# Mamba-2 block and Hadamard feed-forward on one core: ACT's parts of two chunk steps one tile later, squares of a quad by halves, one Hadamard step a tile, dt later

## What is computed

```python
def mamba2(x):                                     # 1024 channels, 16 heads of 64, state of 128
    z, xBC, dt = split(x @ w_in)
    dt = softplus(dt + dt_bias)
    xBC = silu(conv4(xBC) + conv_b)                # causal, 4 taps
    y = ssd(xh * dt, dt * A, Bm, Cm) + xh * D      # Lmat = exp(segsum(dt * A))
    y = y * silu(z)
    y = y * rsqrt(mean(y * y) + 1e-5) * norm_w
    return y @ w_out

xn = layernorm(x)
hidden = fwht(silu(xn @ W1.T) * (xn @ W3.T))       # fwht over 2048, 1/sqrt(2048)
x = x + (xn + mamba2(xn)) + hidden @ W2.T
```

## Time and profile before

| | |
|---|---|
| median of 3 runs | 967.67 us (966.13 to 968.0) |
| profiled execution | 965.39 us, span 963.6 us |
| PE busy | 934.7 us, 97% |
| DVE busy | 555.8 us, 58% |
| ACT busy | 391.4 us, 41% |
| POOL busy | 276.1 us, 29% |

### The profile page before, as it was taken

One profiled execution on the slowest core, in us unless ns is written; L12 is line 12 of the kernel. 1 busy time (PEld: TensorE's weight loads), 2 busy tenths in 40 slices (PEclk: granted clock), 3 DMA queues, 4 the chain that ended last, 5 costly groups with the idle time before them and its releaser, 6 DMA issues.

```text
span 963.6 us, 13435 instructions
## 1 busy us (share of the span) xinstructions
PE 934.7 (97%) x5000; PEld 469.3 (49%) x5000; DVE 555.8 (58%) x955; ACT 391.4 (41%) x690; POOL 276.1 (29%) x354
## 2 busy tenths in 40 slices
PE   9899987989899999999999999999999999999998
PEld 4444443545344445555454445555445445555543
DVE  7876588875534756556532766566451666575421
ACT  6678874533323445233221434233222444343200
POOL 0000446352000116466110106565210104654410
PEclk9999999999999999999999999999999999999999
DMA  9798355434224335525223435436223435256123
GB/s 336 247 349 295 112 192 193 131 124 137 96 74 147 125 111 159 155 72 176 88 67 113 143 99 164 145 97 175 78 76 101 143 107 160 65 151 153 45 77 98
DMA packets 76208, 134.26 MB, mean 139 GB/s; under 512 B 7536, under 2 KB 20464, under 8 KB 74096
## 3 DMA queue, kind: packets, MB, share of 16 engines
q1 hardware_dynamic: 56640, 104.88, 34.1%
q10 hardware_dynamic: 19504, 28.53, 10.0%
HBM read 107.43 MB, written 25.95 MB: 138 GB/s over the span
## 4 chain that ended last, share of the span: by engine, by line
PE 67%; DVE 1%; DMA 1%; ACT 1%; issue 0%; DVEq 0%; ACTq 0%
PE ps L600 46%; PE ps L834 14%; PE ps L796 2%; PE ps L782 1%; PE ps L788 1%; PE ps L768 1%; DMA arena<-cs_rows 1%; PE ps L619 0%; PE ps L638 0%; PE ps L751 0%; PE ps L771 0%; DVE arena L1348 0%; DVE arena L1426 0%; ACT arena L1059 0%; DVE arena L1265 0%
## 5 line engine op out<-in xcount | busy, mean ns | idle before, releaser
L600 PE MATMUL ps<-xh,arena 128*128 128x512 f16 x1592 | 487.9, 379 | 3.4 <-DVE arena L1194 3.3
L600 PE MATMUL ps<-xl,arena 128*128 128x512 f16 x796 | 302.0, 379 | 0.0
L600 PEld LDWEIGHTS ps<-xh,arena 128*128 128x128 f16 x1592 | 158.3, 99 | 190.3 <-issue 5.9
L834 PE MATMUL ps<-arena 128*128 128x512 f16 x768 | 171.1, 379 | 0.0
L1443 POOL TENSOR_TENSOR arena<-arena 128x512 f16<-128x512 f32 x64 | 71.2, 1113 | 334.6 <-ACT arena L978 334.6
L1244 DVE SCALAR_TENSOR_TENSOR arena<-ps,cw,arena 128x511 f32<-128x511 f32 (+2 forms) x120 | 89.4, 747 | 66.9 <-ACT arena L968 65.0
L600 PEld LDWEIGHTS ps<-xl,arena 128*128 128x128 f16 x796 | 77.9, 98 | 88.7 <-issue 3.3
L834 PEld LDWEIGHTS ps<-arena 128*128 128x128 f16 x768 | 74.1, 98 | 91.2 <-issue 5.5
L978 ACT ACTIVATE arena<-arena 128x512 f16<-128x512 f32 x64 | 40.2, 629 | 141.3 <-DVE arena L1265 141.3
L1260 DVE SCALAR_TENSOR_TENSOR arena<-arena,ps 128x512 f32<-128x512 f32 x64 | 44.0, 687 | 77.3 <-ACT arena L973 77.0
L600 PE MATMUL ps<-wo_hi,arena 128*128 128x512 f16 x256 | 79.9, 384 | 3.6 <-DVE wo_lo L1333 3.4
(11 more groups left out here) (179 smaller groups left out, 1092.8 us busy)
## 6 DMA issues: line engine op xcount, KB each, us to landing
arena<-w_parts SPq DMA_DIRECT2D x198, 256.0 KB, 2.6
w_parts<-arena SPq DMA_DIRECT2D x66, 256.0 KB, 2.6
arena<-cs_rows ACTq DMA_DIRECT2D x16, 1024.0 KB, 5.7
arena<-w SPq DMA_DIRECT2D x24, 512.0 KB, 4.9
arena<-ecs_rows ACTq DMA_DIRECT2D x24, 256.0 KB, 6.9
arena<-x ACTq DMA_DIRECT2D x18, 256.0 KB, 3.4
w_mid<-arena SPq DMA_DIRECT2D x8, 512.0 KB, 3.5
arena<-w_mid SPq DMA_DIRECT2D x16, 256.0 KB, 2.6
```

The source lines that it names most:

```text
L600: ins = nc.tensor.matmul(out_ap, lhs(i, a), rhs(i, c), start=(i == 0 and s == 0), stop=(i == n - 1 and s == 2))
L834: ins = nc.tensor.matmul(bank(t), hw[a][:, i, t * P:(t + 1) * P], w2s[i % W2R][:, d, :], start=(i == 0 and s == 0), stop=(i == JF - 1 and ...
```

## The change

Six things, all in batch 0:

- `FIRST`: DT moves from behind Z0 to behind C2, DTL from behind C2 to behind Z1, SUM from behind C4 to behind Z2, ahead of C4.
- An SQ entry is now one half of a quad (two tiles), with its own place; halves of one quad stand one to three tiles apart.
- ACT's part of Y (the square of y) becomes a step of its own, YS, and ACT's part of N (y as fp16) becomes NS, each with its own places in batch 0: mostly one tile behind Y and N. In the other batches they stand at the places of Y and N.
- The Hadamard steps stand at tiles 31 to 46, one a tile; before, H5 and H6 stood at the same tile, and H0 to H4 a tile earlier.
- N and Q of chunk 1 move from tile 20 to tile 21, W of chunk 0 from 18 to 19.
- On PE, QS of quad 6 waits for `mean_read` of chunk 0 instead of `mamba_evac`; W of chunk 0 waits for seven scales (`scale_13`) instead of six; DVE's QS 6 waits for `pe_tot` no more.

```diff
-FIRST = ("B G1S C C0 G1N C1 Z0 DT C2 DTL Z1 C3 Z2 C4 SUM Z3 WOL F0 C5 F1 SQ0 Z4 F2 C6 F3 QS0 Z5 F4 C7 F5 SQ1 Z6 F6 Z7 F7 QS1 E0 A0").split()
+FIRST = ("B G1S C C0 G1N C1 Z0 C2 DT Z1 DTL C3 Z2 SUM C4 Z3 WOL F0 C5 F1 SQ0 Z4 SQ1 F2 C6 F3 QS0 Z5 F4 C7 F5 SQ2 Z6 SQ3 F6 Z7 F7 QS1 E0 A0").split()
...
-            [("H", j, at) for j, at in enumerate((30, 31, 32, 33, 34, 35, 35, 38, 39, 40, 41, 42, 43, 44, 45, 46))])
+            [("H", j, at) for j, at in enumerate(range(31, 31 + JF))])
...
-              "Y": (9, 17, 26, 34), "N": (12, 20, 28, 37), "Q": (12, 20, 28, 37), "V": (14, 23, 30, 39), "W": (18, 25, 31, 41),
+              "Y": (9, 17, 26, 34), "YS": (10, 18, 27, 35), "N": (12, 21, 28, 37),
+              "NS": (13, 22, 29, 38), "Q": (12, 21, 28, 37), "V": (14, 23, 30, 39), "W": (19, 25, 31, 41), "ROW": (15, 24, 31, 40)}
...
                         elif i == 6:
-                            pe.wait_ge(mamba_evac.sem, mamba_evac.at(0, 0))
+                            pe.wait_ge(mean_read.sem, mean_read.at(0, 0))
...
                             pe.wait_ge(wo_l, QE)
-                            pe.wait_ge(scale_13, 6)
+                            pe.wait_ge(scale_13, 7)
...
                     elif kind == "SQ":
-                        act.wait_ge(d_quad[i], 32)
+                        quad, half_of = divmod(i, 2)
+                        act.wait_ge(d_quad[quad], 32)
...
-                        for half_of in range(2):
-                            if i not in (0, QUADS_EARLY):
-                                act.wait_ge(sq_quads, 2 * i + half_of - 1)
...
-                    elif kind == "Y":
+                    elif kind == "YS":
...
-                    elif kind == "N":
+                    elif kind == "NS":
...
                         dve.wait_ge(quad_sums, i + 1)
-                        if i in (4, 6):
-                            dve.wait_ge(pe_tot.sem, pe_tot.at(0, i // 6))
+                        if i == 4:
+                            dve.wait_ge(pe_tot.sem, pe_tot.at(0, 0))
```

More of the change, by code:

```diff
@@ L45 @@
             [("WOH", q, at) for q, at in enumerate((12, 13, 13, 14, 14, 15, 16, 17))] +
[2 rows of a table removed]
+            [("SQ", n, at) for n, at in enumerate((1, 2, 4, 5, 7, 8, 11, 12, 15, 16, 19, 20), 4)] +
+            [("QS", q, at) for q, at in enumerate((3, 7, 12, 14, 18, 23), 2)] +
             [("XL", 0, 18), ("HL", 0, 24), ("W2S", 0, 24)] +
-            [("H", j, at) for j, at in enumerate((30, 31, 32, 33, 34, 35, 35, 38, 39, 40, 41, 42, 43, 44, 45, 46))])
+            [("H", j, at) for j, at in enumerate(range(31, 31 + JF))])
 STEP_FIRST = {"T": (4, 12, 20, 29), "X": (6, 15, 23, 32), "S": (7, 15, 24, 33), "R": (9, 18, 26, 35), "E": (None, 8, 16, 24),
-              "Y": (9, 17, 26, 34), "N": (12, 20, 28, 37), "Q": (12, 20, 28, 37), "V": (14, 23, 30, 39), "W": (18, 25, 31, 41),
-              "ROW": (15, 24, 31, 40)}
+              "Y": (9, 17, 26, 34), "YS": (10, 18, 27, 35), "N": (12, 21, 28, 37),
+              "NS": (13, 22, 29, 38), "Q": (12, 21, 28, 37), "V": (14, 23, 30, 39), "W": (19, 25, 31, 41), "ROW": (15, 24, 31, 40)}
 ES_FIRST = (3, 4, 11, 13, 19, 21, 28, 30)
@@ L62 @@
     "Y": (6, 14, 22, 32),
+    "YS": (6, 14, 22, 32),
     "N": (8, 16, 24, 34),
+    "NS": (8, 16, 24, 34),
     "Q": (8, 16, 24, 34),
@@ L997, in _ @@
                     elif kind == "SQ":
-                        act.wait_ge(d_quad[i], 32)
+                        quad, half_of = divmod(i, 2)
+                        act.wait_ge(d_quad[quad], 32)
                         if i == 0:
                             act.wait_ge(sq_g1, G1_ACT)
-                        elif i == QUADS_EARLY:
+                        elif i == 2 * QUADS_EARLY:
                             act.wait_ge(xt_done.sem, xt_done.at(0, MC - 1))
-                        junk = sq_act[i >= QUADS_EARLY]
-                        for half_of in range(2):
-                            if i not in (0, QUADS_EARLY):
-                                act.wait_ge(sq_quads, 2 * i + half_of - 1)
-                            column = SQ_Q + 2 * i + half_of
-                            nc.scalar.activation(junk[:, half_of * 2 * TILE:(half_of + 1) * 2 * TILE].rearrange("p (s c) -> p s c", s=2),
-                                                 raw_load_view(i, half_of), ACT.Square,
-                                                 accum_out=row_sq[:, column:column + 1]).then_inc(sq_quads, 1)
+                        if quad not in (0, QUADS_EARLY):
+                            act.wait_ge(sq_quads, i - 1)
+                        junk = sq_act[quad >= QUADS_EARLY][:, half_of * 2 * TILE:(half_of + 1) * 2 * TILE]
+                        nc.scalar.activation(junk.rearrange("p (s c) -> p s c", s=2), raw_load_view(quad, half_of), ACT.Square,
+                                             accum_out=row_sq[:, SQ_Q + i:SQ_Q + i + 1]).then_inc(sq_quads, 1)
                     elif kind == "F":
```

## The result

The changed kernel takes 978.4 us (978.15 to 981.03) against 967.66 us (966.13 to 968.0) of the kernel before: a ratio of 1.0118, 95% interval 1.01 to 1.0137, slower by 10.7 us.

The account below looks back on a forecast made before the run. PE was taken as bound, busy 660.01 of 664.00 us from 300 us on, so only its waits in the first 300 us could move. +4.4 - 3.4 - 2.7 + 6.3 + 1.7 = +6.3 on 967.7 gave 974.0 us, range 968.5 to 977.5.

Parts of the forecast that it names:

- Front, +4.4: Start of batch 0: with dt later, the first Hadamard step on raw W2 starts at 58.1 instead of 53.73, +4.4 us.
- Rival 4: Front: ACT and DVE have slack, so its 4.4 is gone by A0; +1.9, 969.6 us, chance 0.06.
- rival 1: Both new idles: only the waits count, no slow stretches behind them; front 2.7, total +2.9, 970.6 us, chance 0.14.
- Middle, -3.4: Middle of batch 0: squares by halves and ACT's later parts of Y and N gain 3.4 us; bounds nothing and -12.2.
- QS4: Middle, sum of squares of a quad on PE: starts near 125.6 instead of 128.88, no slow clock behind it.
- W0: Middle, W of chunk 0 on PE: held by the seventh scale to 160.9 against 160.53, wait 3.7, one tile won.
- rival 3: Middle gives nothing: POOL's long steps hold DVE's wo_lo pieces, seventh scale over 3 later; +9.7, 977.4 us, chance 0.10.
- N2: Middle, N of chunk 2 on PE: its square of y comes only 1.1 earlier, so the gain there is 1.1.
- H0's wait of 2.31: End of the middle, first of the later Hadamard steps: its wait goes, as chunk 3's X times dt comes 2 earlier.
- Tail, +5.3: End of batch 0: two old waits go, -2.7; an idle ahead of the seventh Hadamard step, +6.3; slow clock, +1.7.
- the middle gives back its waits: Rival for the middle: the seventh scale is ready before PE needs it, full 12.2 gained; -2.5, 965.2 us, chance 0.13.

Follow-up runs that it names:

- e1: Changed kernel with DT, DTL and SUM back at their old places in the front; 975.23 us, ratio 1.0095 to the kernel before.
- e2: Kernel before with nothing but DT, DTL and SUM moved to their new places; 972.15 us, ratio 1.0065.
- e4: Changed kernel with W of chunk 0 back at tile 18 with six scales, and QS of quad 6 at tile 20 with its old waits; 978.74 us.
- e5: Changed kernel with N and Q of chunk 1 back at tile 20 and that chunk's y copy one tile earlier; 975.13 us, ratio 1.0075.
- e6: Changed kernel with the Hadamard steps at their old places and the square of y of chunk 3 back at tile 34; 974.21 us, ratio 1.0067.
- e8: Changed kernel with the undoings of e1, e4, e5 and e6 together; squares by halves and ACT's later parts stay; 961.21 us, ratio 0.9934 to the kernel before.
- e11: The e8 version with the square of y and the y copy back at the tiles of Y and N, squares by halves kept; 965.15 us, ratio 0.9985.
- e9: The e8 version with W of chunk 0 again at tile 19 with seven scales and QS of quad 6 at 18; 962.97 us, ratio 0.9952.
- e7: Changed kernel with the next batch's layernorm at tile 37 instead of 35, Hadamard steps still one a tile; 979.73 us, ratio 1.0121.
- e3: Changed kernel with the sixteen Hadamard steps back at their old tiles, square and copy of chunk 3 at their new places; 982.8 us, ratio 1.0173.

## Why the prediction was right in its sign and short in its size

**Front, +4.4: right.** SUM at 49.52 against 49.5, F0 at 58.23 against 58.1, the clock at its lower level behind it, and in e1's trace the whole shift came through to H15. The bounds of 2.7 to 5.0 were too narrow above: e2, e4, e5 and e6 show F0 up to 59.70, since the slow stretch behind the same idle lasts longer in some executions. The table load is shown by itself, as before (from 47.13, with the Ln at 48.42); SUM's start left no room for the further 1.38 us of drain that the Trainium skill counts ("ScalarE: Activation LUTs", "What ACT_TABLE_LOAD costs"). Rival 4, that the front isn't felt, is out by the traces of e1 and e2 and by e2's median. What rival 1 had for it, that the 2.37 ahead of C4 brought no slow clock, was so in that execution, but in e1 the clock was 0.57 from 45 to 49 behind the same wait, and e8 to e11 are like e1. It cost nothing there, as F0's old wait took it up.

**Middle, -3.4: wrong, it was +0.9.** This is where the 4.3 us of the error are. Step by step, times unshifted as in the prediction (less 4.5):
- QS4 came at 127.1 and not at 125.6, with a wait of 1.94 and a slow clock behind it: the gain here was 1.8 instead of 3.3, and the slow clock was to be gone.
- W0 came at 164.4 and not at 160.9, and PE stood 4.7 and not 3.7. The working's structure was right (the last of wo_lo, Y1's two steps, U8, a split, the scale, all in that order), its start was 3.4 late: the last wo_lo piece ended at 159.9 instead of 156.5. The rows of DVE:

```profile
162.85 1.57 DVE L1333 SCALAR_TENSOR_TENSOR wo_lo<-arena,nws,wo_hi 128x512 f16<-128x512 f32 x1
164.35 1.21 DVE L1365 TENSOR_TENSOR arena<-ps,arena 128x1024 f32<-128x1024 f32 x1
...
166.80 0.68 DVE L1265 SCALAR_TENSOR_TENSOR arena<-ps,arena 128x512 f32<-128x512 f32 x1
...
168.68 0.15 DVE L1308 TENSOR_SCALAR f<-inv 128x1 f32<-128x1 f32 x1
```

  A piece of wo_lo takes 0.74 alone; this one took 1.57, an earlier one 1.93, beside long steps of POOL. The last two pieces of the kernel before, however:

```profile
156.27 2.04 DVE L1333 SCALAR_TENSOR_TENSOR wo_lo<-arena,nws,wo_hi 128x512 f16<-128x512 f32 x1 [2.73 <-ACT wo_hi L1037]
...
159.73 0.74 DVE L1333 SCALAR_TENSOR_TENSOR wo_lo<-arena,nws,wo_hi 128x512 f16<-128x512 f32 x1
```

  Together they took 2.78 there and 2.79 here (1.22 and 1.57). So the stretching is mostly not new, and is not shown to be what made the 4 us that the working had for this release into 0.6; 1.5 of it was missing from QS4 on, and the rest was not traced. The stretching is what rival 3 named (with the Trainium skill's "SBUF — State Buffer", "Who interferes with whom", which the rows agree with in that the DVE step grew longer; that it stood still for POOL's is not shown). And e4 shows that in the changed kernel W0's longer wait doesn't reach the end: undone, it leaves N2 where it was to 0.4. Rival 3 gave the nearest time (977.4), but its N2 was to be late with W0, and that is not what held it.
- **The step that failed is N2.** I had it 1.1 earlier, from what W0 wins; it came 3.4 later, and W0 has at most 0.4 of it (e4). The change moves N and Q of chunk 1 by a tile. That edit was listed with the change and never priced in the working: Q1's 1.9 us on DVE slid ahead of U10's eviction, ACT's yh copy ahead of tanh A11, and the exponentials of chunk 2 behind both. Undone alone (e5) it gives 2.4 us back by the trace, 3.4 without the clock's part, 3.3 by the medians, of the 4.5 that N2 was off. The rest is the gain of 1.1 itself. With N1's move undone N2 is 0.9 (e5) and 0.6 (e9) later than before, counted from F0; less what the slow clock behind W0 took (2.7, 2.4, and 1.7 before) it stands where it did, to 0.1. That is an estimate from single executions; in none of them does N2 come 1.1 earlier with W0 at its new place.
- H0's wait of 2.31 went, as said. From N2 to the first G it takes 19.0, or 19.9 with the Hadamard step that moved, against 22.4: 2.5 less. 3.4 less 2.5 is the middle's +0.9.

**Tail, +5.3: right, +5.5.** Wait of 6.41 ahead of H6 against 6.3 worked out, both old waits gone, a slow clock behind it. From 260.5 to 267.5 the granted clock was 0.68, which loses 2.2 and not 1.7. e7 confirms the mechanism, that the idle follows the next Hadamard step behind LN wherever LN stands. e3 shows what the working had missed though it had the instruction in its chain: the square of chunk 3 behind LN's steps holds N3 as well, and would have cost the same idle by itself. The changed kernel pays once for both.

**The other rivals.** That only the waits count (970.6) fell with the clock rows behind both new idles. That the middle gives back its waits (965.2) fell for N2. Without N1's move, W0's, the front's and the tail's, e8 has 2.3 us of gain in the middle, where that rival had counted on 12.2.

## What to carry to other kernels

When a step of a chain is moved by one tile, price each engine's part of it against the tile's own eviction next to it, also where the move looks like making room: here N and Q of one chunk, one tile later, cost about as much (2.4) as the one wait that the change took away in the middle had been worth (2.3). Before chasing the longest wait, ask where PE is held next by a chain that doesn't start there: 1.5 us more of waiting ahead of W0 cost nothing at the end as long as N2 was held by another chain. A single profile can't settle a size of 1 us where the clock differs from the other's; compare what each lost first. And when one step stands behind a long stretch of an engine, look for all its companions that do as well; undoing one of two that share an idle shows nothing, or a loss.
